# A residual attention-and-FFN kernel: all square layers in seven block products, and half of the attention moved into the second chunk

## The reference

```
x = x + attn(layernorm(x))          # per batch: s = n @ ctx^T ; h = gelu_tanh(s) * s ; h @ ctx
n = layernorm(x)
h = silu((n @ w1^T) * s1) * ((n @ w2^T) * s2)      # layer 1: 256 -> 1024
h = gelu((h @ h1^T) * sh1)                         # square layer 0: 1024 -> 1024
h = gelu((h @ h2^T) * sh2)                         # square layer 1: 1024 -> 1024
x = x + (h @ w3^T) * s3                            # layer 4: 1024 -> 256
```

## Time and profile before

| | |
|---|---|
| median of three runs | 341.13 us |
| profiled execution, its own time | 342.24 us |
| its span | 340.4 us |
| TensorE busy | 329.5 us (97%), 1668 matmuls |
| VectorE busy | 256.4 us (75%) |
| ScalarE busy | 202.7 us (60%) |
| granted TensorE clock, mean | 0.997 |

### The profile page before, as it was taken

One profiled execution on the slowest core, in us unless ns is written; L12 is line 12 of the kernel. 1 busy time (PEld: TensorE's weight loads), 2 busy tenths in 40 slices (PEclk: granted clock), 3 DMA queues, 4 the chain that ended last, 5 costly groups with the idle time before them and its releaser, 6 DMA issues.

```text
span 340.4 us, 4764 instructions
## 1 busy us (share of the span) xinstructions
PE 329.5 (97%) x1668; PEld 279.1 (82%) x1668; DVE 256.4 (75%) x476; ACT 202.7 (60%) x334; POOL 33.9 (10%) x65
## 2 busy tenths in 40 slices
PE   7779999999999999999999999999999999999994
PEld 5579888888888888888899888888888888888894
DVE  3567859509966695897779768997988688976684
ACT  2345904275643354867796367669586769576840
POOL 6521025002202100011000000000000000010000
PEclk9999999999999999999999999999999999999998
DMA  5999876991038989434655655536656474443003
GB/s 154 288 376 389 312 235 217 301 393 62 3 110 280 309 301 369 176 123 131 235 168 207 201 182 175 160 141 227 214 190 193 177 272 162 123 126 123 0 13 118
DMA packets 26333, 67.56 MB, mean 198 GB/s; under 512 B 1728, under 2 KB 3136, under 8 KB 24512
## 3 DMA queue, kind: packets, MB, share of 16 engines
q1 hardware_dynamic: 17520, 47.27, 39.6%
q0 software_dynamic: 8784, 19.92, 19.5%
HBM read 56.71 MB, written 10.49 MB: 197 GB/s over the span
## 4 chain that ended last, share of the span: by engine, by line
PE 91%; DMA 5%; POOL 1%; DVE 1%; issue 0%; ACT 0%; SPq 0%; POOLq 0%
PE P L1262 45%; PE P L1325 17%; PE P L1215 15%; PE P L1351 9%; DMA xs<-in_x 3%; DMA W<-in_w 2%; PE P L1163 2%; PE P L1171 2%; PE P L1179 2%; POOL W L487 1%; POOL rs L482 0%; DVE st L793 0%; ACT xt L563 0%; POOL rs L480 0%; DVE st L813 0%
## 5 line engine op out<-in xcount | busy, mean ns | idle before, releaser
L1262 PE MATMUL P<-TR,WR 128*128 128x512 f32 x672 | 152.6, 389 | 0.0
L1262 PEld LDWEIGHTS P<-TR,WR 128*128 128x128 f32 x672 | 126.1, 188 | 26.2
L905 DVE TENSOR_TENSOR TR<-H,TR 128x512 fp32r<-128x512 f32 x84 | 57.4, 688 | 21.0 <-ACT TR L611 18.8
L611 ACT ACTIVATE TR<-H 128x512 fp32r<-128x512 f32 x84 | 52.5, 629 | 22.9 <-DVE H L900 17.3
L1215 PE MATMUL P<-X,W 128*128 128x512 f32 (+1 forms) x320 | 61.4, 349 | 0.1
L1325 PE MATMUL P<-TR,WR 128*128 128x512 f32 x256 | 61.4, 395 | 0.0
L1215 PEld LDWEIGHTS P<-X,W 128*128 128x128 f32 x320 | 51.7, 189 | 8.1 <-DVE X L838 0.5
L1325 PEld LDWEIGHTS P<-TR,WR 128*128 128x128 f32 x256 | 47.7, 188 | 9.7
L601 ACT ACTIVATE SL<-P,sc 128x512 f32<-128x512 f32 (+1 forms) x40 | 24.0, 602 | 27.5 <-PE P L1215 25.4
L878 DVE SCALAR_TENSOR_TENSOR H<-P,sc,SL 128x512 f32<-128x512 f32 (+1 forms) x40 | 25.3, 638 | 15.1 <-ACT SL L601 8.8
L652 ACT ACTIVATE H<-H,sc 128x512 f32<-128x512 f32 x36 | 26.0, 721 | 16.4 <-DVE H L921 16.4
(11 more groups left out here) (70 smaller groups left out, 234.6 us busy)
## 6 DMA issues: line engine op xcount, KB each, us to landing
WR<-in_h POOLq DMA_DIRECT2D x15, 1024.0 KB, 5.4
WR<-blocks_h SPq DMA_DIRECT2D x12, 1024.0 KB, 5.5
H<-in_h SPq DMA_DIRECT2D x8, 1024.0 KB, 10.1
blocks_h<-H SPq DMA_DIRECT2D x8, 1024.0 KB, 7.3
xn<-in_h SPq DMA_DIRECT2D x8, 512.0 KB, 3.7
xt<-in_h SPq DMA_DIRECT2D x8, 512.0 KB, 4.2
W<-in_w POOLq DMA_DIRECT2D x4, 512.0 KB, 6.1
WR<-in_w POOLq DMA_DIRECT2D x2, 1024.0 KB, 5.5
```

What stands on the lines that cost most here:

```text
L611: eng.activation(TR[:, f % RING, 0, :], operand(c, L, s, kk), ACT.Copy).then_inc(s_hi, 1)
L905: eng.tensor_tensor(TR[:, f % RING, 1, :], operand(c, L, s, kk), TR[:, f % RING, 0, :].bitcast(f32), ALU.subtract).then_inc(s_lo, 1)
L1262: out_ = eng.matmul(bank(c, L, s, m)[:, :], WR[r % WRING][:, at:at + 128], TR[:, f % RING, h, :], start=(s in FRESH and kk == 0 and h == 0 ...
```

## The change

Square layer 0 of chunk 0 is now done in seven products as well. Their order in layer 0 of both chunks is 0, 5, 1, 2, 3, 4, 6. Products 0 and 5 share four banks and stand between layer 1 of the two token halves, in both chunks; the other five follow the second half. Product 0 is snapped, product 5 is added on top of it in the same banks and goes through gelu straight from PSUM; `put_back` (new, ScalarE) copies the kept product 0 back into banks before product 2. `early_products` and `late_products` are the engines' streams for this, in place of `eight`. h1's sums are now formed first (raw 0 to 3), h2's (raw 4 to 7, two of them in a buffer that SL and Y share) after it. The attention of batches 4 and 5 is spread over layer1(1), square layer 1 and layer 4 of chunk 0, that of 6 and 7 over layer1(2) and the early products of chunk 1. Most of the weight tests move into chunk 1. In the diff, b = 4c + 2 in `early_products`; `added` is a wait on s_cd, `kept` one on s_sn; the pieces come in the order GpSimd, ScalarE, VectorE, TensorE.

```
-FRESH = (0, 1, 5)
+ORDER = {0: (0, 5, 1, 2, 3, 4, 6), 1: (0, 1, 2, 3, 4, 5, 6)}
+FRESH = {0: (0, 1), 1: (0, 1, 5)}
...
+TURN = ((4, 5, 6, 7, 0, 1), (6, 7, 0, 1, 4, 5))
+TURN0 = (6, 7, 0, 1, 4, 5)
+FIRST = (0, 1, 4, 5)
+SETS = ((6, 7, 0, 1), (2, 3, 4, 5))
...
-            load_w8(0)
-            load_w8(1)
-            load_w8(2)
-            rstds(2, (1, 1), (0, 2), (0, 3))
-            load_w8(3)
-            rstds(5, (1, 2), (1, 3), (0, 4), (0, 5))
-            load_w8(4)
-            rstds(9, (1, 4), (1, 5), (0, 6), (0, 7))
-            load_w8(5)
+            rstds(2, (1, 1))
+            load_w(0, 0, 0)
+            rstds(3, (0, 2))
+            load_w(0, 0, 5)
+            rstds(4, (0, 3), (1, 2), (1, 3), (0, 4), (0, 5))
...
+            def put_back(c, m):
+                consumed_last(eng, 2 * c + 1, SETS[0][m])
+                eng.activation(bank(c, 0, 2, m)[:, :], tile(target(c, 0), (1, 0), m), ACT.Copy).then_inc(s_pre, 1)
...
+            def late_products(c):
+                for i in range(4):
+                    put_back(c, i)
+                    hi(c, 0, 2, i)
+                    if i == 2 and (c, 0, 1) in BESIDE:
+                        magnitude(BESIDE[c, 0, 1])
+                for s, nxt in ((2, 3), (3, 4)):
                     for i in range(4):
-                        gelu8(7, i)
+                        snap(c, 0, s - 1, i)
+                        hi(c, 0, nxt, i)
+                        if i == 2 and (c, 0, s) in BESIDE:
+                            magnitude(BESIDE[c, 0, s])
+                for i in range(4):
+                    hi(c, 0, 6, i)
+                    gelu(c, 0, (0, 1), i)
+                    if i == 2 and (c, 0, 4) in BESIDE:
+                        magnitude(BESIDE[c, 0, 4])
+                for i in range(4):
+                    gelu(c, 0, (1, 1), i)
+                    hi(c, 1, 0, i)
+                    if i == 2 and (c, 0, 6) in BESIDE:
+                        magnitude(BESIDE[c, 0, 6])
...
+            def late_products(c):
+                add_up(c, 0, 2)
+                if c == 1:
+                    test(BESIDE[1, 0, 1])
+                for i in range(4):
+                    lo(c, 0, 3, i)
+                for i in range(4):
+                    add(c, 0, 6, i)
+                if c == 0:
+                    combine(4)
+                else:
+                    test(BESIDE[1, 0, 2])
+                add_up(c, 0, 4)
+                if c == 0:
+                    combine(5)
+                else:
+                    test(BESIDE[1, 0, 3])
+                for i in range(4):
+                    total(c, 0, (0, 1), i)
+                    lo(c, 0, 6, i)
+                if c == 0:
+                    combine(6)
+                    combine(7)
+                else:
+                    test(BESIDE[1, 0, 4])
+                for i in range(4):
+                    total(c, 0, (1, 1), i)
+                    lo(c, 1, 0, i)
+                if c == 1:
+                    test(BESIDE[1, 0, 6])
...
+            def early_products(c):
+                b = 4 * c + 2
+                gate(b)
+                gate(b + 1)
+                for i in range(4):
+                    lo(c, 0, 5, i)
+                if c == 0:
+                    combine(0)
+                else:
+                    test(5)
+                resid(b)
+                resid(b + 1)
+                scale(1, b)
+                scale(1, b + 1)
+                if c == 0:
+                    combine(1)
+                else:
+                    test(6)
+                second(b)
+                second(b + 1)
+                if c == 0:
+                    combine(2)
+                else:
+                    test(7)
...
+                        if m == 0:
+                            combine(3)
+                        if m in (1, 2):
+                            stats(0, 3 + m)
+                        if m in (3, 4):
+                            scale(0, 1 + m)
+                    if t % 2 == 1 and m % 2 == 0:
+                        add(t // 2, 0, 1, m // 2)
...
-                    if c == 0 and k in (3, 5):
-                        last(c, 1, k // 4)
-                    if c == 0 and k in BESIDE4:
-                        test(BESIDE4[k])
+                    if c == 0 and k in (0, 1):
+                        last(c, 1, k)
+                    if c == 0 and k in (4, 5):
+                        resid(k)
+                    if c == 0 and k in (6, 7):
+                        scale(1, k - 2)
+                if c == 0:
+                    second(4)
+                    second(5)
...
+                if L == 0:
+                    if s == 0:
+                        consumed_last(eng, 2 * c, FIRST[m])
+                    if s == 5:
+                        kept(eng, c, 0, 0, m)
+                    if s == 1:
+                        if m >= 2:
+                            consumed_last(eng, 2 * c + 1, SETS[1][m])
+                        elif c == 0:
+                            eng.wait_ge(s_xt, 5 + m)
+                        else:
+                            eng.wait_ge(s_X1, 7 + m)
+                    if s == 2:
+                        eng.wait_ge(s_pre, 4 * c + m + 1)
+                    if s == 3:
+                        kept(eng, c, 0, 1, m)
+                    if s == 4:
+                        kept(eng, c, 0, 2, m)
+                    if s == 6:
+                        added(eng, c, 0, (1, 1), m)
...
+                if (t, i) == (1, 10):
+                    turn(0, 4)
+                    turn(0, 5)
...
+            def attend4(half, k):
+                if (half, k) == (1, 1):
+                    score(4)
+                    score(5)
+                if (half, k) == (0, 0):
                     weigh(4)
                     weigh(5)
-                if (t, i) == (1, 10):
+                if (half, k) == (0, 7):
                     turn(1, 4)
                     turn(1, 5)
...
-            layer1(0)
-            eight(0)
-            layer1(1)
-            eight(1)
             for c in range(NC):
-                if c:
-                    square(c, 0)
-                square(c, 1)
+                layer1(2 * c)
+                product(c, 0, 0)
+                product(c, 0, 5)
+                layer1(2 * c + 1)
+                for s in ORDER[0][2:]:
+                    product(c, 0, s)
+                for s in ORDER[1]:
+                    product(c, 1, s)
```

643 lines of the change are left out of this document (256 added, 387 removed).

## The result

The kernel after takes 376.14 us (median of 4 runs, 375.32 to 377.62), the kernel before 341.56 (4 runs beside it): ratio 1.102 (95% interval 1.097 to 1.106). The direction was right, the size not: +34.6 us where +18.6 was forecast, 9 us beyond the range. Ratios are of runs in the fast state; one of the 15 runs of the kernel before that stand beside the last version took 476.86 us at a granted clock of 0.657 and is left out of its ratio.

A forecast was written before the change was run, and what follows sets the result against it. TensorE was taken to set the time, with VectorE nearly full. Terms -7.25 - 1.45 + 2.8 + 11.7 + 2.2 + 3.65 + 6.9 = +18.55 gave 360.8 us profiled, 359.7 median; range 348 to 367.

The forecast's parts named there:

- Removed: Chunk 0: one product of eight fewer, 32 matmuls at 226.7 ns; -7.25 us.
- The start: Start of kernel: later weight loads let x land before VectorE asks, transpose at 23.3 in place of 24.75; -1.45 us.
- layer1(1): TensorE waits 1.75 and 1.0 us for scaled batches 4 and 5 from VectorE's unbroken queue; +2.8 us.
- Product 6 of chunk 0: VectorE's queue ends at P+70.7 (P: product 0's start), costing 5.8 us; the total-to-total chain costs 5.9; +11.7 us.
- The forecast's own sign: Late products of chunk 0: VectorE idle for more than some 3 us would mean its queue was counted too long.
- The clock behind product 6's waits: Chunk 0: TensorE's standing still lowers the clock, so product 6's first microseconds run slower; +2.2 us.
- Layer 4: In chunk 0, TensorE waits 2.0 us for lo, and layer1(2) waits for second(5); +3.65 us.
- Chunk 1: Before product 6, VectorE reaches the total between on time (5.9) and 1 us late (7.4); +6.9 us.
- Rival (b): The clock falls in chunk 1 too, during steps of 2.15 us idle and 0.45 busy; 361.9 us, 10%.
- (a): VectorE keeps up in chunk 0: queue's 5.8 us and its cold clock don't come, chain's 5.9 stay twice; 351.7 us, 15%.
- (c): The weight sums are late: three 1 MB loads share engines, TensorE waits 3 us more; 362.7 us, 6%.
- (d): Faster: the four totals keep to 1.2 us and product 6 is late by under a microsecond; 338.9 us, 5%.

The follow-up runs named there:

- experiment 9: All orders at once, plus combine(6), combine(7) ahead of the four lo and the second sum's load ahead of two looks; 349.85 us (1.024).
- Experiment 2: Kernel after, with raw 6 asked for ahead of raw 7 on SyncE; 373.54 us (1.091).
- experiment 5: Kernel after, with combine(6) and combine(7) of chunk 0 behind the four totals and lows on VectorE; 370.46 us (1.083).
- experiment 1: Kernel after, with hi ahead of the gelu on ScalarE in block (1, 1) of both chunks; 366.40 us (1.070).
- Experiment 6: Kernel after, without the five weight looks beside the late products of layer 0 in chunk 1; 370.20 us (1.081).
- experiment 11: Last version: experiments 8 to 10 built on, looks moved, sums' loads ahead of them, four hi of product 6 ahead of the gelus; 340.29 us (0.994).
- experiments 8 to 10: Kernel after with all orders at once, 349.49 us; then the sums of h2 sooner, 349.85; then more small waits edited, 348.71.
- experiment 4: Kernel after, with turn(0, 4) and turn(0, 5) at step 14 of layer1(1) in place of 10; 371.96 us (1.087).

## Why the prediction was wrong

By its steps, forecast and measured in the profiled execution:

- Removed: -7.25. The count fell by 32 matmuls, as predicted; 226.7 ns for each is the forecast's price.
- The start: -1.45 forecast, -2.4 measured (the transposes behind the wait start at 22.34, before at 24.75). The wait of 1.92 went whole, where I left some 0.5. The other 0.5 is luck: it was there ahead of the wait (layer 1's run of 36 matmuls starts at 17.66, before at 18.16), and in experiment 9 it isn't (18.10, the transposes at 22.78).
- layer1(1): +2.8 forecast. The waits are 1.94 and 1.24 us, forecast as 1.75 and 1.0. Not forecast: the clock went down behind them, and the 20 matmuls after them took 7.0 us where 4.5 is their time at 226.7 ns. +3.2 +2.5, the 2.5 being the worst of seven profiles.
- Product 6 of chunk 0: +11.7 forecast; 16.2 measured (from 105.07, the 103.70 of product 4's end and three banks more, to 121.29). **This is the step that failed.** It laid VectorE's work end to end and said "That ends at P+70.7"; the totals start at P+77.3 (112.75). 4.1 of the difference is the wait for raw 6, a term that the forecast put at nothing: its list has "two combines (5.0)" and no transfer ahead of them. It priced such transfers only for h1's sums, "out 4.1 to 4.9, back in 4.7 or more"; here the way out took 9.34 us and the way in 7.65, with three to four megabyte transfers in flight and the engines' share at 1.0. Experiment 2 puts 2.5 us of raw 6's own time on its neighbours, experiment 5 shows that the whole wait is this queue. Most of the other 2.5 came down from layer1(1)'s cold stretch; it moved product 4's end as well (68.3 in place of 66.2), so it isn't in the 16.2. The forecast's own sign, VectorE idle for more than 3 us here, did come, and for the opposite reason: the queue was counted too short. The chain's 2.60 per bank was right to the digit, and experiment 1 shows it apart.
- The clock behind product 6's waits: +2.2 forecast, 2.7 to 3.0 measured (59.69 against 56.96 with fillers, or 56.67 at 226.7 ns).
- Layer 4: +3.65 forecast, 2.9 of waits measured (3.2 by the stretch: 23.82 where the forecast has 20.6 as ideal).
- Chunk 1: +6.9 forecast; +0.8 in product 1, then 10.5 at product 6 (286.07 to 296.54) and 2.5 of clock: 13.8. **By size this is the larger miss**, 6.9 us against 4.5 in chunk 0. "Between on time and 1 us late" was some 4.6 late (10.5 less the 5.9 of on time): the magnitudes hold up `hi` (its `lo` waits up to 1.26), and the tests fill the queue. Experiment 6, where VectorE is on time, takes 4.5 us of it. Rival (b) is true as far as it goes, +2.5 for its 2.2.

The measured terms are -7.25 - 2.4 + 5.7 + 16.2 + 3.0 + 2.9 + 13.8 = +32.0 of the span's +35.4. The other 3.4 I have not placed in full. About half of it is in the waits: two matmuls behind one take 0.70 to 0.74 us at full clock (experiments 6 and 11) where 0.45 is their time, and six of the waits above are counted without that. The rest is no matter of the clock: the same sum for experiment 11, 340.4 - 7.25 - 2.4 + 4.4 = 335.2, leaves as much of its 338.8.

The price for the transfers could have been read more safely before. The earlier trace rows show one quiet transfer; the page of the kernel before has the medians of all eight, raw weights in and sums out:

```profile
H<-in_h SPq DMA_DIRECT2D x8, 1024.0 KB, 10.1
blocks_h<-H SPq DMA_DIRECT2D x8, 1024.0 KB, 7.3
```

Of the rivals, (a) is out: VectorE did not keep up. (b) happened together with the forecast. (c) is out: the three loads were asked for at 63.3 and no wait for a sum shows. (d) is out for this order, and its condition wasn't enough: in experiments 8 to 10 product 6 starts 0.7 to 1.2 us late, near what it asks for, and they take 349.5, 349.9 and 348.7 us where it has 338.9. Only with the looks out of ScalarE's way is the kernel at 340.3. My range treated the rivals as alternatives. Four terms leaned the same way, late queues and a cold clock, and the range should have held their sum. They don't need one another: product 6's wait is 9.53 without those of layer1(1) (experiment 4), and the clock falls in chunk 1 without the wait of 4.12 (experiment 6).

What stays open: what decides the clock's loss in layer1(1). The same two waits were followed by 0.50 over 68:72 in the kernel after, 0.75 there in experiment 1 and 1.00 in experiment 5, with the same instructions up to then. Open too: what the seven products of this layer are worth by themselves.

## What to carry to other kernels

When an edit takes away the work between a bank's last use and its next, list for each of the four instructions between (total, gelu, `hi`, `lo`) what stands ahead of it in its queue and doesn't belong to it; here two swapped lines were worth some 8 us, more than the product removed. A copy for a check, or a transfer out and back in through one buffer, costs nothing until the engine whose queue it stands in is the late one; price transfers by how many are in flight then, not by a quiet row. And add to waits of TensorE of over a microsecond that come in a row the chance of up to 3 us lost at half clock behind them.
